# The last layer's bias as an addition to the input residual on GpSimd instead of a product on TensorE

## The reference

```python
out_nr = _gelu(x @ w1_nr + b1_nr) @ w2_nr + b2_nr            # condition 0
out_tsr = _gelu(x @ w1_tsr + b1_tsr) @ w2_tsr + b2_tsr       # condition 1
out_sr = _gelu(_gelu(x @ w1_sr + b1_sr) @ w2_sr + b2_sr) @ w3_sr + b3_sr   # condition 2
y = x + out                # nothing is added to x for another condition
y = layernorm(y) * gamma + beta
h = _gelu(y @ down_W.T + down_b)
h = h @ expert_W[domain].T + expert_b[domain] + domain_emb[domain]
result = layernorm(h @ up_W.T + up_b + y) * ln_gamma + ln_beta
```

## Time and profile before

| | us |
|---|---|
| median of 3 runs | 301.08 (300.67 to 301.18) |
| profiled execution, its time | 299.47 |
| profiled execution, span from first to last instruction | 297.4 |
| TensorE busy | 267.8 (90%) |
| ScalarE busy | 204.9 (69%) |
| VectorE busy | 198.5 (67%) |
| GpSimd busy | 149.8 (50%) |

### The profile page before, as it was taken

The page is one execution under the profiler, slowest core; times in us unless marked ns, Lnnn a source line. Parts: engine busy times, 40 slices in busy tenths (PEclk is TensorE's granted clock), DMA queues, the critical chain, the costliest instruction groups (busy, mean ns, idle before and its releaser), DMA issues.

```text
span 297.4 us, 8345 instructions
## 1 busy us (share of the span) xinstructions
PE 267.8 (90%) x1999; PEld 252.7 (85%) x2000; DVE 198.5 (67%) x668; ACT 204.9 (69%) x451; POOL 149.8 (50%) x164
## 2 busy tenths in 40 slices
PE   1899997999999999899999999999999999959720
PEld 1578997999999998799999999999999999958510
DVE  6667622318546645697888878888788888856571
ACT  3376675876877775788787887878888878836410
POOL 3203724544655746456564555655556546525433
PEclk9999999999999999999999999999999999999775
DMA  7830310100211221122233422324223242311112
GB/s 208 222 95 17 67 35 2 39 21 20 56 46 46 53 71 35 49 75 71 71 97 81 105 71 71 97 69 116 71 71 96 66 121 71 87 43 39 53 44 62
DMA packets 43807, 21.00 MB, mean 71 GB/s; under 512 B 37754, under 2 KB 42025, under 8 KB 43721
## 3 DMA queue, kind: packets, MB, share of 16 engines
q1 hardware_dynamic: 41142, 13.95, 20.2%
q0 software_dynamic: 1584, 4.33, 4.1%
q10 hardware_dynamic: 1060, 2.45, 2.9%
HBM read 12.02 MB, written 8.65 MB: 70 GB/s over the span
## 4 chain that ended last, share of the span: by engine, by line
PE 81%; issue 8%; DMA 3%; POOL 2%; DVE 2%; ACT 1%; POOLq 1%; ACTq 0%; DVEq 0%
PE ps_h L828 19%; PE ps_z L897 10%; PE ps_u L933 9%; PE ps_d L1071 9%; PE ps_z L902 5%; PE ps_z L863 5%; PE ps_t L914 5%; PE ps_u L863 4%; PE ps_u L801 3%; DMA per_unit_sb<-in_per_unit 3%; PE ps_t L984 3%; PE ps_z L885 3%; PE ps_t L987 3%; PE ps_t L985 3%; POOL rs L410 1%
## 5 line engine op out<-in xcount | busy, mean ns | idle before, releaser
L405 POOL TENSOR_TENSOR h_lo<-h,h_hi 128x256 fp32r<-128x256 f32 (+1 forms) x75 | 70.3, 938 | 104.3 <-ACT h L716 104.3
L716 ACT ACTIVATE h_hi<-ps_h,per_feature_sb 128x256 fp32r<-128x256 f32 x84 | 38.2, 480 | 25.9 <-PE ps_h L828 25.8
L410 POOL TENSOR_TENSOR rs<-ve,minus_half 128x4 f32<-128x4 f32 x36 | 40.5, 1124 | 27.7 <-DVE ve L585 27.6
L573 DVE BATCH_NORM_STATS2 st<-ps_z 128x6 f32<-128x256 f32 x66 | 24.8, 415 | 37.5 <-PE ps_z L902 37.5
L421 POOL DMA_INDIRECT out<-o,out_rows_now x33 | 35.1, 1063 | 6.6 <-issue 5.6
L732 ACT ACTIVATE yt<-ps_t,per_feature_sb 128x256 f32<-128x256 f32 x66 | 34.0, 572 | 6.3 <-PE ps_t L914 6.3
L723 ACT ACTIVATE zn<-ps_z,nm,rs 128x256 f32<-128x256 f32 x66 | 33.7, 561 | 6.6 <-DVE nm L589 6.0
L716 ACT ACTIVATE h<-ps_h,per_feature_sb 128x256 f32<-128x256 f32 x84 | 38.1, 482 | 0.0
L933 PE MATMUL ps_u<-table_hi,stack 128*128 x132 | 36.4, 306 | 1.4 <-DVE stack_hi L668 1.4
L1071 PE MATMUL ps_d<-yt,per_feature_sb 128*128 128x256 f32 x132 | 35.0, 388 | 3.0 <-DVE out_rows L661 1.8
L933 PE MATMUL ps_u<-table_lo,stack_hi 66*128 x132 | 33.8, 286 | 0.0
(11 more groups left out here) (148 smaller groups left out, 698.4 us busy)
## 6 DMA issues: line engine op xcount, KB each, us to landing
x<-in_x_feat SPq DMA_DIRECT2D x130, 64.0 KB, 2.2
out<-o SPq DMA_DIRECT2D x66, 64.0 KB, 2.0
last_sb<-in_last_w ACTq DMA_DIRECT2D x1, 768.0 KB, 5.8
per_unit_sb<-in_per_unit ACTq DMA_DIRECT2D x1, 593.1 KB
out<-o,out_rows_now POOLq DMA_INDIRECT x33, 2.8
w_sr_sb<-in_w_sr SPq DMA_DIRECT2D x1, 512.0 KB, 3.7
w_two_sb<-in_w_two SPq DMA_DIRECT2D x1, 512.0 KB, 4.6
w_sr_sb<-in_w_sr ACTq DMA_DIRECT2D x1, 512.0 KB, 3.9
```

The costliest lines, as they stand in the source:

```text
L405: pool.tensor_tensor(dst, full, high.bitcast(F32), ALU.subtract).then_inc(ready, 1)
L410: pool.tensor_tensor(RS[p][:, :, :], VE[p][:, :, :], mhalf[:, :].rearrange("p (n t) -> p n t", n=2), ALU.pow).then_inc(rstd, 1)
L716: ins = act.activation(dst[:, m, :], src[m], ACT.Gelu, bias=COL[:, bass.ds(col + m, 1)])
```

## The change

The bias of the last layer is no longer a product. GpSimd adds it to the input in feature layout, where it is one number for each partition: `XB[:, c, :] = XF[:, c] + bias`, two instructions of 128x256 a slot, and TensorE's input residual transposes `XB` in place of `XF`. `XB` is a single buffer. The additions stand at the start of step g on GpSimd, for slot g + 1, and wait for `x_hi` of that slot and for the residual of slot g; a ladder of comparisons chooses the column of the kind. TensorE's residual waits for `xb_made`. The loads of SP wait for `x_lo` and `xb_made` in place of `x_used`. `LBH`, `ones2`, their memsets, casts, DMAs and semaphores go; the biases come with `per_feature`, 8 columns wider.

```diff
@@ sync @@
-            sp.wait_ge(s_lb, 1)
-            sp.wait_ge(s_lbh_zero, 1)
-            for row, half in enumerate((LB_HI, LB_LO)):
-                sp.dma_start(LBH[row:row + 1, :].bitcast(F32), half[:, :].bitcast(F32)).then_inc(s_lb_low, 16)
...
-                    sp.wait_ge(x_used, g + 2)
+                    sp.wait_ge(x_lo, g + 2)
+                    sp.wait_ge(xb_made, g + 2)
@@ gpsimd @@
-            pool.memset(LBH[:, :].bitcast(F32), 0.0).then_inc(s_lbh_zero, 1)
...
+            def biased_input(slot, p, where):
+
+                pool.wait_ge(x_hi, slot + 1)
+                if where != HEAD or slot > 0:
+                    pool.wait_ge(xb_used, slot)
+                pool.sem_inc(x_seen, 1)
+                with pool.If(slot < b_sr):
+                    add_bias(SR, p)
+                with pool.Else():
+                    with pool.If(slot < b_nr):
+                        add_bias(NR, p)
+                    with pool.Else():
+                        with pool.If(slot < b_tsr):
+                            add_bias(TSR, p)
+                        with pool.Else():
+                            add_bias(OTHER, p)
+
+            def add_bias(kind, p):
+
+                for c in range(KC):
+                    col = COL_B3 + KC * kind + c
+                    ins = pool.tensor_scalar(XB[:, c, :], flat(XF[p][:, c, :, :]), COL[:, col:col + 1], None, ALU.add)
+                ins.then_inc(xb_made, 1)
...
+            pool.wait_ge(s_feat_in, 16)
...
+                for slot in on_slot(pool, g, -1, where, n_slots):
+                    biased_input(slot, 1 - p, where)
                 for slot in on_slot(pool, g, 0, where, n_slots):
                     with pool.If(g < b_sr):
                         low(h2l[:, :, :], h2[:, :, :], h2h[:, :, :], h2_full, h2_lo, g)
@@ vector @@
-            step(dve.memset(ones2[:, :].bitcast(F32), 0.0))
-            dve.memset(ones2[0:2, :].bitcast(F32), 1.0)
...
-            dve.memset(LB[:, :], 0.0).then_inc(s_lb_zero, 1)
...
-            dve.wait_ge(s_lb_in, 16)
-            step(dve.tensor_copy(LB_HI[:, :], LB[:, :]))
-            dve.tensor_tensor(LB_LO[:, :], LB[:, :], LB_HI[:, :].bitcast(F32), ALU.subtract).then_inc(s_lb, 1)
@@ scalar @@
-            act.wait_ge(s_lb_zero, 1)
-            act.dma_start(LB[0:OTHER, :], last_b).then_inc(s_lb_in, 16)
@@ tensor @@
-                    pe.wait_ge(x_lo, g + 2)
+                    pe.wait_ge(xb_made, g + 2)
...
-                    residual(ZP[q], input_tile(q)).then_inc(x_used, 1)
+                    residual(ZP[q], lambda t, c: XB[:, c, t * P:(t + 1) * P]).then_inc(xb_used, 1)
...
-                if first:
-                    pe.wait_ge(s_lb_low, 32)
-                pe.matmul(ZP[p][:, :, :], ones2[:, :],
-                          LBH[:, bass.ds(kind * H, H)].unsqueeze(1).to_broadcast([P, TT, H]),
-                          start=False, stop=False)
```

More of the change, by code:

```diff
@@ L128, in conditioned_layers @@
         XL = [sb(f"x_lo{p}", [P, KC, G, T], F32R) for p in range(2)]
+        XB = sb("x_biased", [P, KC, N])
         h1 = sb("h1", [P, 2 * KC, N])
@@ L398, in _ @@
             ins.then_inc(s_zero_last, 1)
-            pool.memset(LBH[:, :].bitcast(F32), 0.0).then_inc(s_lbh_zero, 1)
-            b_sr, _, _, n_slots = bounds(pool)
+            b_sr, b_nr, b_tsr, n_slots = bounds(pool)
             def low(dst, full, high, made, ready, g):
@@ L1010, in finish_sr @@
                 weights_ready(where, g, "last")
-                last_layer(SR, lambda: None, lambda: pe.wait_ge(h2_lo, g + 1), p,
-                           where == HEAD and g == 0)
+                last_layer(SR, lambda: None, lambda: pe.wait_ge(h2_lo, g + 1), p)
                 with pe.If(g + 1 < b_sr):
@@ L1022, in finish_other @@
                     weights_ready(where, g, "last")
-                    last_layer(kind, lambda: pe.wait_ge(h1_hi, g + 1), lambda: pe.wait_ge(h1_lo, g + 1), p,
-                               where == HEAD and g == 0)
+                    last_layer(kind, lambda: pe.wait_ge(h1_hi, g + 1), lambda: pe.wait_ge(h1_lo, g + 1), p)
                 start_two(g, 1 - p, where)
@@ L1103 @@
     expert = v["L1_cond_expert_W"].transpose(1, 0, 2)
-    last_b = np.stack([v["L0_cond_b3_sr"], v["L0_cond_b2_nr"], v["L0_cond_b2_tsr"]])
     per_unit = np.zeros((A + 1, H + 2 * E + 2 * A * E), np.float32)
```

24 lines of the change are left out of this document (7 added, 17 removed).

## The result

| | before | after |
|---|---|---|
| median of the runs | 301.13 (300.67 to 301.37) | 324.24 (322.82 to 325.57) |
| profiled execution: time, span | 299.47, 297.4 | 325.57, 323.5 |
| granted clock of TensorE, mean | 0.975 | 0.948 |

The ratio after to before is 1.0758, 95% interval 1.0727 to 1.0789. The change made the kernel 7.6% slower. The forecast was 297.4, the range ended at 304; 324.2 lies even beyond rival 2, whose 313.5 went with X = 0.73.

A forecast was written before the change was run, and what follows sets the result against it. TensorE was taken as the bound, never idle through the steps. SR steps +1.4, other kinds -4.6 and the end -0.5 sum to -3.7 us: 301.08 - 3.7 = 297.4 us, range 293.5 to 304 for 8 in 10.

The forecast's parts named there:

- rival 2: GpSimd becomes the bound, additions costing like the two-input form, X = 0.73: +12.4 us, 313.5 us; chance 0.26.
- X: Time of one 128x256 GpSimd addition, two a slot: taken as 0.42 us, with 0.34 and 0.73 as ends.
- The formula for the other steps: Non-SR steps: store ends 4.49 us after the residual, 1.53 more needed; step 6.02 us, -4.6 us for 22 steps.
- The ladder, 0.25: Register operation, wait and compare-and-branches on GpSimd ahead of the additions, taken as 0.25 us.
- The collision, 0.39: Non-SR steps: additions meet VectorE's `o` and `stack`; 0.39 us added for `stack` to go first.
- The SR loop through GpSimd: SR steps: loop of 9.99 us plus 1.14 for the additions makes 11.13 from slot 6 on; phase +1.4 us.
- The head at 0: Kernel start: removed zeroing, casts, bias DMAs and waits costed at nothing, since TensorE's work covers them.
- The end at -0.5: Last two slots, beside a 3.19 us TensorE wait that stays: their two removed products give -0.5 us.
- The product's 0.27 us: Removed bias product on TensorE: 0.27 us in each of 33 slots, 8.9 us in all.

The follow-up runs named there:

- experiment 4: Changed kernel with one 128x512 GpSimd addition a slot, first half's bias column for both halves, in place of two of 128x256; 325.44 us in one run.
- experiment 5: Changed kernel with one two-input GpSimd addition of 128x512 a slot, bias column spread over the row, in place of two one-input additions; 337.31 us, ratio 1.1153.
- experiment 3: Changed kernel with GpSimd's additions adding the constant 0.0 in place of the bias column; 315.88 us, ratio 1.0471 to the kernel before.
- Experiment 9: Changed kernel with TensorE's input residual in SR steps moved from ahead of the expert products to behind the last layer; 311.37 us, ratio 1.0318.
- Experiment 7: Kernel without any bias (no product, no additions), GpSimd's last subtraction of step 1 made to wait for `nm`; 295.89 us, ratio 0.9806.
- experiment 1: Changed kernel without GpSimd's additions, residual reading `XF`, so no bias at all; 298.53 us, ratio 0.9884 to the kernel before.

## Why the prediction was wrong

- **X, the price of an addition: this step failed.** It was taken by form from the select and the iota, 0.42 us, and bounded above by the two-input subtraction, 0.73. Measured are 1.06 us on average and 2.02 for a pair in the steps. The bound rested on "one input instead of two" being cheaper; experiments 3 to 5 show that the one-input form of GpSimd is the dearer: 512 columns take 1.07 us on average with two inputs (one of them spread), 1.69 with one (at least 1.57). The slope was the wrong one: a column of the addition costs 2.4 ns (experiment 4), where the select had given 1.2 and the iota 0.8; the subtraction's is 2.3. The Trainium skill's rule (GPSIMD Engine Reference, 4.1 Engine selection) that one-input work is roughly at line rate speaks for the forecast's side; here the measurement decides against it.
- **The formula for the other steps: right on average.** 4.49 us from the residual to the store's end, as read from the earlier trace rows, and with what was measured behind it, 0.05 + 2.02 + 0.05, give 6.61. Measured are (281.79 - 142.53)/21 = 6.63. That the two agree so well is partly luck: the store ends by turns 4.57 and 4.23 us behind the residual, and only behind the former does TensorE wait. Rival 2 had the mechanism and its sign, "each 0.1 us on X costs 5.2"; it ended at X = 0.73.
- **The ladder, 0.25: too dear**, 0.05. **The collision, 0.39 before the additions: not as a delay.** It stands in the durations of both engines: `o` 561 ns and `stack` 548, where they were 478 and 433, the casts 373 for 285.
- **The SR loop through GpSimd: right in kind.** Its 9.99 us with the measured 2.11 (0.05 + 2.01 + 0.05) give 12.10; the first two distances are 12.38 and 12.41. **Missed was the clock.** The third and fourth are 13.9. The forecast had TensorE idle 0.8 us a step and gave no price to idleness. For 0.8 us that was right: in experiment 5 TensorE waits 0.70 to 0.75 us in these steps and the granted clock is 1.00 throughout, and even at 1.5 us (experiment 3) it is. So the clock's loss too came with the wrong X. Experiment 9 shows the loss gone with the wait; that the clock's part was 1.5 us a step is read from the changed kernel's rows.
- **The head at 0: missed.** Not the removed casts, but a race of `nm` with GpSimd's subtraction and the clock behind the longer wait. Experiment 7 shows it for the kernel without bias (1.1 us in that step, 2.6 in the medians); the mend was not run on the changed kernel itself, so its share in the 2.25 us of the table is read from the same stall of 3.12 us, not shown.
- **The end at -0.5: missed**, +2.0, with a granted clock of 0.50 behind a wait that both kernels have. Why the clock fell in one and not in the other is open.
- **The product's 0.27 us: right in the step** (10.33 and 5.99, experiment 1), worth 5.6 us in the total of experiment 7 instead of 8.9. Of the missing 3.3 a good 2 lie in the head there (slot 4's residual at 64.39, 1.5 later than before, where 0.8 sooner was due), the rest in steps of the other kinds of 6.05 us on average.

The sum over again, with what was measured in the steps, a pair of additions in 2.02 us and so X = 1.01: 0.59 more on X make 30.7 us, less what ladder (0.20 x 26 = 5.2) and collision (0.39 x 22 = 8.6) had too much, so the forecast's -3.7 becomes +13.2. The head adds 3.1 to that (2.25 instead of -0.8), the clock three times 1.5 in the SR steps, the end some 2. These some 23 us stand against 26.1 between the two spans. Of the other 3 most lies in the SR stretch, whose loop is 0.3 us a step longer than 12.10 and whose last residual, slot 10's, waits 0.81 us; no run separates these.

## What to carry to other kernels

An instruction that the trace has never shown has no upper bound from one that looks dearer: measure it alone before a sum multiplies it by 52. Moving work to an idle engine is paid by the place of its reader: here the kernel with the same additions was 23 us slower than the one before with an early reader and 3 with a late one. And a wait in an engine that had been full can cost its clock besides its length, but not every wait does: here 1.75 us in each SR step did from the second on, 1.5 us did not.

## What the runs showed of the hardware

- GpSimd's addition of a number for each partition took 1.06 us on average for 128x256, at least 0.92 (0.945 on average with a constant), while its subtraction of two tensors of that size took 0.73.
- For 128x512 the one-input addition took 1.69 us on average, the addition of a column spread over the row 1.07 to 1.09, the subtraction of two full tensors 1.31.
- VectorE's two-input `stack` took 1.86 us instead of 0.42 beside a two-input addition of GpSimd, 0.80 at the same place beside a one-input addition of that size, and 0.42 beside the store alone.
- Three waits of TensorE of nearly the same length, 1.74, 1.76 and 1.75 us, 12.4 and 13.9 us apart: granted clock 1.00 behind the first, 0.72 over six us behind the others. Three of 1.52, 1.52 and 1.50 us, 12.15 us apart (experiment 3): 1.00 throughout. The waits of 0.16 to 0.81 us between 142.5 and 281.8 us of the changed kernel: 1.00 as well.
- VectorE's `nm`, 128x2, took 0.16 or 1.22 us, as it started ahead of a GpSimd subtraction or 0.06 us behind it.
